# Warm-up and filling products of TensorE recounted, and the condition's weights loaded in two halves at the head of both queues

## The reference

```python
x: (64, 64, 1024) f32            # b, c, t
W = weights[condition]           # weights (16, 64, 64), condition (64,) int32
h = einsum('bct,bcd->bdt', x, W) # the condition's product
xf = h.reshape(4096, 1024)
scores = xf @ Wr.T               # (4096, 64)
top_vals, top_idx = top_k(scores, 16); gates = softmax(top_vals)
G = zeros(4096, 64).at[arange, top_idx].set(gates)
hid = einsum('nd,krd->nkr', xf, A)                 # A (64, 16, 1024)
out = x + 2.0 * einsum('nkr,kdr->nd', hid * G[:, :, None], B)   # B (64, 1024, 16)
```

## Time and profile before

| what | value |
|---|---|
| median of three runs | 723.25 us |
| profiled execution | 722.8 us, span 721.0 us |
| TensorE busy (PE) | 713.0 us, 99% |
| weight loads (PEld) | 600.1 us, 83% |
| VectorE (DVE) | 488.3 us, 68% |
| ScalarE (ACT) | 262.2 us, 36% |
| GpSimd (POOL) | 37.6 us, 5%, all of it in the first 70 us |
| moved by DMA | 178.41 MB, mean 247 GB/s |

### The profile page before, as it was taken

The page is one execution under the profiler, slowest core; times in us unless marked ns, Lnnn a source line. Parts: engine busy times, 40 slices in busy tenths (PEclk is TensorE's granted clock), DMA queues, the critical chain, the costliest instruction groups (busy, mean ns, idle before and its releaser), DMA issues.

```text
span 721.0 us, 9267 instructions
## 1 busy us (share of the span) xinstructions
PE 713.0 (99%) x3444; PEld 600.1 (83%) x3444; DVE 488.3 (68%) x953; ACT 262.2 (36%) x499; POOL 37.6 (5%) x30
## 2 busy tenths in 40 slices
PE   9999989999999999999999999999999999999998
PEld 8888878788888888888888888888888888888886
DVE  4698999797545698855443769866534286797652
ACT  5567762444424432133231543122332264223200
POOL 1873000000000000000000000000000000000000
PEclk9999999999999999999999999999999999999999
DMA  9958359955895776474767675846666787545663
GB/s 325 406 196 345 125 197 417 346 215 227 296 332 195 298 258 236 172 267 175 285 248 262 234 291 191 292 163 217 253 238 241 260 290 273 195 146 194 223 226 145
DMA packets 56158, 178.41 MB, mean 247 GB/s; under 512 B 9650, under 2 KB 9778, under 8 KB 55602
## 3 DMA queue, kind: packets, MB, share of 16 engines
q1 hardware_dynamic: 54386, 174.09, 66.8%
q10 hardware_dynamic: 1728, 3.74, 1.4%
HBM read 131.66 MB, written 46.14 MB: 247 GB/s over the span
## 4 chain that ended last, share of the span: by engine, by line
PE 91%; DVE 6%; DMA 2%; ACT 0%; issue 0%; POOL 0%; SPq 0%; POOLq 0%
PE Pb L267 40%; PE Pb L249 37%; PE Cb L229 7%; PE S L283 4%; DVE Cq L365 2%; DMA xc<-in_x 2%; DVE Wt L200 1%; DVE Op L182 1%; PE T L522 1%; DVE R L365 1%; PE T L300 0%; PE T L355 0%; DVE Op L545 0%; DVE Q L365 0%; DVE Xo L182 0%
## 5 line engine op out<-in xcount | busy, mean ns | idle before, releaser
L249 PE MATMUL Pb<-Op,Wt 128*128 128x512 f32 x1008 | 238.3, 392 | 2.4 <-DVE Op L182 1.9
L249 PEld LDWEIGHTS Pb<-Op,Wt 128*128 128x128 f32 x1008 | 187.5, 188 | 41.4 <-DVE Op L182 2.5
L267 PE MATMUL Pb<-Wt,Op 128*128 128x512 f32 x912 | 212.0, 391 | 0.0
L267 PEld LDWEIGHTS Pb<-Wt,Op 128*128 128x128 f32 x912 | 170.1, 188 | 34.5
L365 DVE TENSOR_TENSOR Q<-Pb,Q 128x512 f32<-128x512 f32 x112 | 77.3, 690 | 87.8 <-PE Pb L267 87.8
L267 PE MATMUL Pb<-Wt,Ox 128*128 128x512 f32 x432 | 100.8, 391 | 0.0
L267 PEld LDWEIGHTS Pb<-Wt,Ox 128*128 128x128 f32 x432 | 80.5, 188 | 16.3
L235 ACT COPY R<-Cb 128x512 f32<-128x512 f32 x60 | 35.2, 587 | 161.3 <-PE Cb L229 161.2
L182 DVE TENSOR_TENSOR Op<-R,Op 128x512 fp32r<-128x512 f32 x98 | 70.1, 739 | 19.1 <-ACT Op L180 19.1
L365 DVE TENSOR_TENSOR Cq<-Pb,Cq 128x512 f32<-128x512 f32 x64 | 43.9, 686 | 40.9 <-ACT Cq L376 30.9
L249 PE MATMUL Pb<-Ox,Wt 128*128 128x512 f32 x288 | 66.3, 389 | 0.0
(11 more groups left out here) (90 smaller groups left out, 463.9 us busy)
## 6 DMA issues: line engine op xcount, KB each, us to landing
Wt<-Wd SPq DMA_DIRECT2D x168, 512.0 KB, 4.8
Wd<-Wt SPq DMA_DIRECT2D x56, 512.0 KB, 5.0
Q<-in_x SPq DMA_DIRECT2D x32, 512.0 KB, 5.0
xc<-in_x SPq DMA_DIRECT2D x24, 512.0 KB, 4.3
out<-Q SPq DMA_DIRECT2D x32, 256.0 KB, 2.6
out<-Q SPq DMA_DIRECT2D x16, 512.0 KB, 2.9
BR<-in_B SPq DMA_DIRECT2D x3, 1024.0 KB, 8.3
BR<-in_x SPq DMA_DIRECT2D x11, 256.0 KB, 11.6
```

The source lines that it names most:

```text
L249: t = pe.run(lambda e, c=c, o=o, a=a, z=z: e.matmul(Pb[:, b, :], Wt[:, k, a, 128 * c:128 * c + 128], part(o, z), start=fresh and (c, a, z) ...
L267: t = pe.run(lambda e, c=c, o=o, k=k, a=a, z=z: e.matmul(Pb[:, b, :], part(o, a)[:, 128 * i:128 * i + 128], Wt[:, k, z, :], start=fresh an ...
```

## The change

Two constants and one load. WARM goes from 20 to 12 and FILL from 6 to 7. The load of Wa becomes two, each of 64 partitions and 256 KB: the lower half stays the first DMA of ScalarE's queue, the upper half becomes the first of SyncE's queue, ahead of the condition numbers and of x. Both count on the same semaphore, and VectorE waits for the sum of both.

```diff
-WARM = 20
-FILL = 6
+WARM = 12
+FILL = 7
...
-        t_wa = ac.load(l_xc[0], lambda e: e.dma_start(Wa, wts))
+        ac.load(l_xc[0], lambda e: e.dma_start(Wa[0:64], wts[0:64]))
+        t_wa = sp.load(l_xc[0], lambda e: e.dma_start(Wa[64:128], wts[64:128]))
         cn = sp.load(l_cn, lambda e: e.dma_start(cnd[:, :], cond.rearrange("(a b) -> a b", a=1)))
         load_x0(sp, 0, 1)
         load_x0(sp, 1, 1)
```

## The result

The changed kernel takes 725.2 us (median of 7 runs, 724.66 to 727.16) against 723.25: a ratio of 1.0032, 95% interval 1.002 to 1.0045. It is slower: the medians are 1.95 us apart, and the ratio, taken over all runs, makes it 2.3 (1.4 to 3.3). I had forecast no change, 722.0 to 724.0. The profiled execution took 725.2 as well, with a span of 723.4 against 721.0.

A forecast was written before the change was run, and what follows sets the result against it. TensorE, busy 713.0 of 721.0 us, was taken as the bound. A surviving lead of 0.05 plus 0.1 from earlier loads gave 0.15 us less than 723.25: 723.1, no change, range 722.0 to 724.0.

The forecast's parts named there:

- The warm-up: Kernel start: removing 16 fast passes saves 1.8 us, so the condition's first product can start near 6.5 instead of 8.3.
- The weights in two halves: First loads: two queues from the start bring 0.1 us earlier; bounds 0.65 us later and 0.5 us earlier.
- (b): Second pair's input: x rows 128 to 255 land at 8.1, leaving TensorE idle 0.7 us after the first pair.
- (c): ScalarE's casts in order: A's tile 1 lands at 10.8, so the fourth pair's remainder ends at 12.77.
- The cover of the numbers: VectorE's wait for weights and condition numbers: arriving 0.3 to 1 us later would still cost nothing.
- The clock: After the shorter warm-up: the level has just risen to 2.4 GHz when the condition's products start, so cost nothing.
- Rival 3: Condition's products to first FFN groups: the clock's rise fails, passes take 1.9 times as long; 725.6 us, chance 0.06.
- the gap of 1.9 us "left the level alone": TensorE's earlier idle gaps of 0.47 and 1.9 us did not lower its clock; argument against the clock failing.
- Filling products: Before the first FFN group: one more takes 0.22 us, hidden in 0.3 to 0.4 us of remaining idle.
- The lead dies beside GpSimd: VectorE beside GpSimd's sums of A, to 52 us: of 0.94 us lead only 0.05 passes.
- The lock rule: VectorE with two SBUF inputs and GpSimd exclude each other for a whole instruction; by it the gain is 0.05 us.
- not to split over disjoint halves: Weights load: both halves share the same engines, so the split's term would be 0 instead of -0.1 us.

The follow-up runs named there:

- cnd_first: The changed kernel with the condition numbers loaded ahead of the half of the weights on SyncE's queue; 724.67 us, ratio 1.0031.
- gap12: The kernel before with 12 warm-up products, its first condition product also waiting for x rows 384 to 511; 726.29 us.
- gap20: The kernel before, 20 warm-up products kept, its first condition product also waiting for x rows 384 to 511; 724.26 us.
- fill7: The kernel before with 7 filling products instead of 6; 722.78 us, ratio 0.9997.
- warm12: The kernel before with 12 warm-up products instead of 20, loads and filling products as before; 722.36 us, ratio 0.9988.
- nosum12: The kernel before with 12 warm-up products and GpSimd's twelve sums S3, S2 and S4 left out; 721.82 us, ratio 0.999.
- split20: The changed kernel's loads in two halves alone, with the old 20 warm-up and 6 filling products; 723.56 us, ratio 1.0008.
- warm12b: Repeat of warm12 (12 warm-up products, otherwise the kernel before) in a later session; 722.36 us, ratio 0.9994.
- nosum20: The kernel before with 20 warm-up products and GpSimd's twelve sums S3, S2 and S4 left out; 722.49 us, ratio 0.9996.

## Why the prediction was wrong, point by point

- **The warm-up: right.** The 24 passes ended at 6.1 (forecast about 6.5), with the clock up. That it was up so early is this execution's: the rise came at 5.1 here, and anywhere from 4.3 to 7.4 in the thirteen traces, where I had taken 6.4 for fixed.
- **The weights in two halves: this step failed.** "Bytes ahead of each later item, over both queues, are the same sum, so by bytes the landings of (b) and (c) do not move", with 0.65 us later as the outer bound. In the first 6 us the landings do not follow the bytes: the DMAs start one after another over both queues, and each one more ahead moves the start of those behind it, the 256-byte one too (3.9 to 5.1 to 5.5). x rows 0 to 127 landed 3.0 us later, the second rows 2.05, A's tile 1 1.6. I had the earlier trace rows and read them as bandwidth; the first packets of the two queues' large loads, 1.7 us apart (1.8 and 3.5), could have warned. x rows 0 to 127 had no row in the prediction at all: I asked what is late next of all inputs but this one.
- **The cover of the numbers: failed with it.** They landed at 5.8 instead of 2.0, and VectorE's copies started 1.4 us later, beyond the "0.3 to 1 us" that I had held free. The late copies cost nothing here, as the block weights of pair 0 were ready at 7.6 and x only at 8.7; the numbers' place cost by delaying x (cnd_first).
- **The clock: this step failed too.** The prediction costed it at nothing because it has just risen. It had. It fell at 8.6, in an idle time of 2.7 us that the prediction had at 0.7, and cost 1.6 us: the term at nothing is the largest of the loss. Rival 3 named the clock, with a chance of 0.06, and the wrong mechanism: not a rise that fails but a fall in the idle time that the late x makes; gap12 against gap20 shows that such idle time does it with nothing loaded late, for 2.0 us. That its 725.6 is so near the 725.2 is luck: its own terms, 4.8 less 0.9, make 3.9 and so 727.1, and the fall ended before the first FFN groups, which the rival had at the low level.
- **That the gap of 1.9 us "left the level alone"** held in the trace that the prediction read and in nine others; in three of the thirteen it did not (see below). It was no proof that a gap is safe.
- **Filling products: right** (fill7).
- **The lead dies beside GpSimd: right in place, off in size.** There was no lead in the changed kernel to test it on; warm12 shows idle at 35.1 and 51.6, and nosum12 shows that without GpSimd's sums neither is there. 0.38 us passed 52 instead of 0.05. The lock rule of the Trainium skill's "SBUF — State Buffer", section "Who interferes with whom", fits both: 1.770 us each beside GpSimd's sums, 0.686 without them.
- **The rule of the Trainium skill's "DMA: Bandwidth & Descriptors", section "Rules for kernel authors", that I weighed** (not to split over disjoint halves) pointed the right way. By split20 it was worth 0.5 us, where I had drawn 0 from it.

Open: why the first DMAs begin one after another, why x then took 3.2 us from its first packet in the changed kernel and 1.4 in cnd_first, and whether cnd_first's slow executions are all falls of the clock.

## What to carry to other kernels

At the start of a kernel look at the order in which the DMAs start over all queues, not only at the bytes ahead of an input, and put first what the first product waits for; a load cut in two can make the ones behind it late, the small ones too. A warm-up has to reach to the moment when its successor's data is there, with that moment's own change taken in; ask of every input of the first product, not only of those that were late before. Here twelve products with the loads untouched are the fastest version that leaves no sum out: 722.36 twice, 0.6 to 0.7 below before, though only one of the two intervals is clear of no change.

## What the runs showed of the hardware

- The clock can also fall in the middle of the kernel, just behind the wait of 1.9 us near 90, which all thirteen profiled executions have. warm12b's, by stretch:

```profile
85.00:91.60 6.60, 4.75 (x21) 1.00 0.40 160
91.90:95.10 3.20, 3.20 (x10) 0.50 0.81 317
```

  Ten passes where the kernel before had 15 in the same stretch. gap12's and nosum12's profiled executions show the same, the other ten do not. nosum20's falls at 131 instead, in a wait of 2.3 us for xc; it took 724.35 against that kernel's median of 722.49.
- The rise came at 4.3 to 7.4 us in the thirteen profiled executions, by the pass spacing or the granted clock; TensorE's work began at 1.3 in all. The Trainium skill's "TensorE: Matmul & The Clock Gate", section "What's actually happening", says that it varies, by half a microsecond either way; the spread here is 3.1 us. By the traces it moves the first FFN group of kernels with 20 products and x in time from 12.85 (nosum20) to 13.86 (before) and 14.12 (fill7).
